# Writing out GpSimd's message gathers of a graph layer, with their index columns read in place

## The reference, cut to what matters

```python
xn = layernorm(x)
def mlp(h): return relu(h @ w1 + b1) @ w2 + b2
msgs = mlp(xn[dst])                                   # edge_index = (src, dst); row = src, col = dst
agg = segment_sum(msgs, src, num_segments=3125)
x = x + mlp(xn + agg) + mix(xn)                       # mix: second-order kernel attention, 8 heads
x = x + moe(layernorm(x))                             # 16 experts, best 2 of each node
```

## Time and profile before

| what | value |
|---|---|
| runs, median | 1540.83 to 1543.50 us, 1543.14 us |
| profiled execution, its own time | 1546.45 us |
| its span (first to last instruction) | 1544.5 us |
| TensorE's mean granted clock | 0.855 |
| gathers L719, first and last start | 434.8 and 1075.0 us |
| message matmuls L1805, last start | 1087.0 us |
| additions L1269, last start | 1089.1 us |

### The profile page before, as it was taken

The page is one execution under the profiler, slowest core; times in us unless marked ns, Lnnn a source line. Parts: engine busy times, 40 slices in busy tenths (PEclk is TensorE's granted clock), DMA queues, the critical chain, the costliest instruction groups (busy, mean ns, idle before and its releaser), DMA issues.

```text
span 1544.5 us, 26303 instructions
## 1 busy us (share of the span) xinstructions
PE 1125.4 (73%) x7084; PEld 769.8 (50%) x7085; DVE 947.2 (61%) x2221; ACT 476.4 (31%) x1280; POOL 955.1 (62%) x1069
## 2 busy tenths in 40 slices
PE   2978878888846677667686767776884499999900
PEld 2656534333323444334453444444784499999800
DVE  4998989999955545445454555545356534433366
ACT  1555325555502223223222222221332032322302
POOL 4598339999976666666766667666000367755416
PEclk8999988999977878688877888878996699999955
DMA  5001000000034443444444455455462222222293
GB/s 154 26 26 34 21 21 1 0 0 0 0 102 119 130 131 117 128 132 122 129 124 129 127 153 156 128 155 123 128 219 93 81 69 70 73 70 70 61 236 100
DMA packets 57119, 145.11 MB, mean 94 GB/s; under 512 B 11117, under 2 KB 24909, under 8 KB 56944
## 3 DMA queue, kind: packets, MB, share of 16 engines
q0 software_dynamic: 33488, 101.80, 22.7%
q1 hardware_dynamic: 23584, 42.74, 9.4%
HBM read 124.91 MB, written 19.59 MB: 94 GB/s over the span
## 4 chain that ended last, share of the span: by engine, by line
PE 39%; DVE 18%; another core or an unknown queue 11%; POOL 11%; issue 10%; DMA 3%; DVEq 3%; ACT 2%; SPq 1%; POOLq 0%; ACTq 0%
PE bank L1805 8%; PE bank L2057 8%; PE bank L2068 7%; POOL big L698 6%; DVE node_buf L1269 3%; DVE big L1196 3%; POOL big L641 2%; DVE big L1195 2%; PE bank L1971 2%; PE bank L1858 2%; PE bank L1866 2%; DVEq L1269 2%; DMA x_buf<-x 1%; DMA big<-xn_rows 1%
## 5 line engine op out<-in xcount | busy, mean ns | idle before, releaser
L719 POOL DMA_INDIRECT big<-msg_rows,big x416 | 422.9, 1017 | 212.7 <-issue 102.0
L1269 DVE TENSOR_TENSOR node_buf<-node_buf,bank 125x256 f32 x416 | 174.6, 420 | 301.0 <-remote 131.1
L1805 PE MATMUL bank<-big 128*128 128x256 bf16 x1248 | 218.7, 324 | 63.1 <-DVE node_buf L1269 43.2
L1805 PEld LDWEIGHTS bank<-big 128*128 128x128 bf16 x1248 | 131.8, 114 | 141.3 <-DVE node_buf L1269 65.9
L1196 DVE TENSOR_SCALAR big<-bank,big 125x416 bf16<-125x416 f16 x400 | 184.6, 480 | 0.8 <-PE bank L1678 0.8
L954 ACT ACTIVATE big<-bank 128x500 f32<-128x500 f32 (+1 forms) x208 | 109.2, 572 | 222.8 <-remote 121.9
L698 POOL TENSOR_TENSOR big<-big 125x512 f32<-125x512 f32 x150 | 170.4, 1173 | 5.1 <-PE bank L1750 2.5
L1048 ACT ACTIVATE mid<-bank,const 128x128 f32<-128x128 f32 x256 | 73.0, 368 | 208.7 <-PE bank L2057 193.0
L1678 PE MATMUL bank<-big 125*128 125x416 bf16 x400 | 105.8, 350 | 29.9 <-DVE big L1196 19.6
L2068 PE MATMUL bank<-big,mid 128*128 x512 | 121.0, 380 | 0.0
L759 POOL DMA_INDIRECT moe_rows<-mid,const x64 | 71.7, 1120 | 78.7 <-DVE mid L1585 75.0
(11 more groups left out here) (307 smaller groups left out, 2119.2 us busy)
## 6 DMA issues: line engine op xcount, KB each, us to landing
big<-L_ffn_w SPq DMA_DIRECT2D x32, 512.0 KB
big<-msg_rows,big POOLq DMA_INDIRECT x416
big<-moe_rows SPq DMA_DIRECT2D x10, 560.0 KB
msg_rows<-big SPq DMA_DIRECT2D x25, 187.5 KB
xn_rows<-mid POOLq DMA_DIRECT2D x5, 625.0 KB, 5.8
x_buf<-x SPq DMA_DIRECT2D x5, 560.0 KB
big<-xn_rows SPq DMA_DIRECT2D x5, 560.0 KB
out<-big SPq DMA_DIRECT2D x5, 560.0 KB
```

Source lines behind the costliest of these rows:

```text
L719: pool.indirect_dma_start(msgs[k], None, msg_rows, bass.IndirectOffsetOnAxis(idx_ring[:, half, k:k + 1], 0)).then_inc(msgs_in[k], 16)
L1269: dve.tensor_tensor(rows, rows, agg_ps[2 * half + j][0:P, :], ALU.add).then_inc(s.agg_add, 1)
L1805: last = mm(agg_ps[k % 4], hot_src[:, turn, k, :], msgs[slot][:, D * i:D * i + D], start=i == 0, stop=i == 2, skip_group_check=True)
```

## The change

The index ring, its copies, their semaphore, the loop, the register thresholds and the extra increments go. The 416 gathers are written out one after the other; gather n reads column n of `edge_idx` and waits for the constant n-15 on `agg_mm` (from n = 16 on). Slots, their number, the order of the gathers, what they move and the semaphores they set stay. Buffers allocated behind the ring move down by 32 words of each partition.

```diff
-        self.msg_idx_ok = sem("msg_idx_ok")
-        idx_ring = b.take([2, 2 * GB], I32)
...
-            def gather(n, half):
-                pool.tensor_copy(idx_ring[:, half, :], edge_idx[:, bass.ds(n * 2 * GB, 2 * GB)]).then_inc(s.msg_idx_ok, 1)
-                pool.wait_ge(s.msg_idx_ok, n + 1)
-                for k in range(2 * GB):
-                    if not at(n, (0,)):
-                        pool.wait_ge(s.agg_mm, n * 2 * GB + k - (2 * GB - 1))
-                        apart(pool)
-                    pool.indirect_dma_start(msgs[k], None, msg_rows,
-                                            bass.IndirectOffsetOnAxis(idx_ring[:, half, k:k + 1], 0)).then_inc(msgs_in[k], 16)
-            gather(0, 0)
-            gather(1, 1)
-            with pool.Fori(1, NBATCH // 4) as i:
-                gather(i * 2, 0)
-                gather(i * 2 + 1, 1)
+            for n in range(NQ):
+                if n >= 2 * GB:
+                    pool.wait_ge(s.agg_mm, n - (2 * GB - 1))
+                pool.indirect_dma_start(msgs[n % (2 * GB)], None, msg_rows,
+                                        bass.IndirectOffsetOnAxis(edge_idx[:, n:n + 1], 0)).then_inc(msgs_in[n % (2 * GB)], 16)
```

## The result

The kernel after takes 1520.16 us, the median of four runs (1519.15 to 1521.68), beside 1543.27 us for the kernel before in the same session. The ratio is 0.9856, with a 95% interval of 0.984 to 0.9873. The change makes the kernel 1.4% faster, some 23 us. I had forecast 1543 us, between 1536 and 1549: wrong, and on the slow side. The profiled execution of the kernel after took 1519.15 us itself, with a span of 1517.3 us.

What follows compares the result with a forecast made beforehand. The ring of TensorE, ScalarE and VectorE was taken as the bound, with GpSimd's time hidden behind it. Every term was 0 on the path, so 1546.45 us profiled, or 1543 us in terms of the median, range 1536 to 1549.

Steps and rivals of the forecast that it cites:

- the one on cover: In the gather stage, gathers issued 12 messages ahead leave at least 8 us of cover, so GpSimd savings give 0.
- What bounds the kernel: In the 654 us gather stage, the ring of TensorE, ScalarE and VectorE sets the pace; GpSimd keeps pace behind it.
- Landing: Time from a gather's start until its rows arrive: at most 10.7 us, against 19 us before TensorE takes them.
- Copies and their semaphore: 26 index copies on GpSimd, 0.78 us for each of 25 between gathers: 20.0 us of GpSimd time, 0 on the path.
- Register thresholds, `apart` and the loop: The 0.30 us between gathers stays; at most 120 us of GpSimd time, taken as 0, and 0 on the path.
- Index columns read in place, buffers moved: Gathers read `edge_idx` directly: 0, at most 30 us of hidden GpSimd time; buffers shifted by 32 words: 0.
- The longer program: 352 more gathers in GpSimd's written-out code, up to three more fetch packets: taken as 0, upper end 8 us.
- Rival B: GpSimd stalls fetching the written-out code while gathers run: 8 to 21 us slower, 1556 us; chance 0.06.
- Rival A: The gathers are the path after all, so all of 20.0 us is won: 1523 us; chance 0.10.
- Rivals C and D: C: TensorE's rhythm shifts 5 us either way, 0.09 each; D: GpSimd's waits take longer, still 1543, within the forecast's 0.66.

Runs made afterwards that it cites:

- z_apart: The kernel after with the separate increment put back behind each wait, on chip 2: 1453.95 us, ratio 0.9855 to the kernel before.
- z_after: The kernel after, unchanged, run again on chip 2: 1454.63 us, ratio 0.9878 to the kernel before.

## Why the prediction was wrong

The step that failed is the one on cover: "On the path it is worth 0, because the message has 8 us of cover or more; what hides it is the 12 messages of lead." The lead was read rightly and is still there. But a lead in messages says only that TensorE isn't waiting for data. It doesn't say that GpSimd's time is free. In the kernel before, on a late chip, GpSimd's stream of indirect DMAs holds back the counts for which VectorE, ScalarE and GpSimd wait. Some come in while gathers run; others come in a pause, about a microsecond after its start, and then GpSimd restarts, the others work, and the next burst runs. GpSimd's restart is a link of that ring. The plain transfers (1321 us) and the memsets show that the close row of indirect DMAs makes the lateness; that GpSimd's restart costs time is shown by the increments, 13.3 us. That it does so by way of the held counts is read from the rows; no run shows it by itself.

Point by point:

- *What bounds the kernel.* "So 'remote' here is most simply TensorE finishing later than its matmul records show" was right as to the sender. "The bound is thus the ring of TensorE, ScalarE and VectorE, and GpSimd keeps pace behind it" was wrong: without the indirect DMAs that ring does the kernel in 1321 us. 177 us of the chain under an unknown name should have kept me from a chance of 0.66.
- *Landing.* At most 10.7 us; it is 3.0 us in the median and 8.2 us at most on prompt chips. The bound held. The 19 us from a gather to its matmuls were right too: 18.8 us in the median of the kernel before, 6.6 us at the least. On a late chip the term played no part.
- *Copies and their semaphore.* Taken at 0 on the path, with 20.0 us if there is no cover. Measured: some 4 us on a late chip (not resolved by the intervals), 8.0 us on a prompt one. The 0.78 us read from the earlier trace rows was right for the pair of copy and increment, and I put all of it down to the copy.
- *Register thresholds, `apart` and the loop.* The gap of 0.30 us does belong to the gather: it is unchanged in 324 rows. But I priced the increment from gathers that do not wait. Behind a wait that has held, it delays the gather by 0.5 us (before, and with `apart` alone, against 0.02 us after). The paragraph did allow for a part that shrinks, up to 120 us of GpSimd's time, but said that "on the path both ends give 0". This is the mis-sized term: 0 in the sum, 13.3 us measured.
- *Index columns read in place, buffers moved.* 946 ns in both kernels: right.
- *The longer program.* Right at 0: two more packets, no gap above 0.3 us under "issue". Rival B is out; its price had a slip (the middle of 8 and 21 us is 14.5, not 13), which changes nothing. The rule of the Trainium skill ("Runtime: NRT & Kernel Launch", section "Instruction fetch mechanics") on streamed code, which stood beside it, isn't contradicted.
- *Rival A* had 1523 us and came nearest, by a sum whose parts were others: it gave the copies 20.0 us and the increments nothing, so that it came within 3 us is luck. Its picture, gathers for which TensorE waits, isn't what the first chip's trace shows, but it is exactly what the prompt chips show. Its chance of 0.10 was too small. I held "GpSimd's own 106 us of slot waits, which can't exist if it is the one waited for" against it; they can, if the count that ends them is late because of GpSimd.
- *Rivals C and D.* Clock 0.874 against 0.855 in the profiled executions. The 13.3 us of the increments came at one and the same mean clock; how much of the rest of the gain the clock carries wasn't separated. D is out: waits got cheaper.

Of the 21 us on chip 10, 13.3 us are the increments; with some 4 us for the copies about 4 us are left for the loop and its registers, and for the copies acting together with the increments. No run separates these: the loop without increments and copies wasn't tried, and the copies and the increments were put back on different chips (7 and 10). Also open is by what mechanism indirect DMAs hold back TensorE's counts, and why they do so on some chips and not on others. The runs show when it happens, not how.

## What to carry to other kernels

Before calling an engine's time hidden, say what its instructions do to others while they run, and treat a large unknown sender in the chain of waits as a suspect, not as a name for the engine one would like it to be. Price an instruction between a wait and the work it guards by a row in which that wait really held, not by rows in which it passed at once. Where GpSimd gathers back to back, put the wait directly ahead of the gather with nothing in between, and compare variants on the same chip, since the base itself moved by 5% from one chip to the next.

## What the runs showed of the hardware

- While GpSimd issued indirect DMAs one behind another, semaphore counts of TensorE reached other engines up to some 5 us after the matmuls' ends (464.79 to 470.23 us above), in four sessions of six; in the other two they arrived within 0.02 us. With plain transfers on the same queue the counts arrived within 0.02 us on a late chip too, and with every second one plain 330 of 338 were on time.
- A gather of 128 rows costs GpSimd 0.946 + 0.30 = 1.25 us, one of 64 rows 0.900 + 0.30 us, and it lands after 3.0 and 2.7 us (medians, prompt chips): from 128 to 64 rows GpSimd saves 46 ns, so nearly all of the cost is per gather. 416 x 1.25 = 520 us of the stage of 546 us (434.0 to 980.0) on a prompt chip are this.
- An increment between a wait and an indirect DMA delays the gather by 0.5 us when the wait has held, and by nothing when it hasn't (1.25 us from gather to gather in z_apart as in z_after).
- The same kernel takes 1542 to 1551 us in four sessions and 1473 to 1474 us in two, each on a chip of its own, and the same change gives 0.985 to 0.988 on both, by different parts.
